# Cross-attention in a Perceiver layer: the value products of two groups done together in every second group

## What is computed

```python
x = x + _L0_xattn_ref(_layernorm(x), ctx_768, mask, Wq, Wk, Wv, Wo)   # x 32x64x512, ctx 32x512x384
    q = x @ Wq;  k = context @ Wk;  v = context @ Wv                  # 16 heads of 32
    attn = softmax(where(mask, q k^T * scale, -max))
    out = (attn @ v) @ Wo
x = x + _L0_attn_ref(_layernorm(x), ...)                              # causal self-attention with rope
x = x + _L0_ffn_ref(_layernorm(x), ...)                               # top half of the tokens, gelu, scatter
```

## Time and profile before

| | us |
|---|---|
| median of 3 runs | 1207.1 |
| the execution that was profiled | 1205.95 |
| its span, first to last instruction | 1204.2 |
| PE busy | 1184.5 (98%) |
| DVE busy | 752.1 (62%) |
| ACT busy | 623.7 (52%) |
| POOL busy | 600.5 (50%) |

### The profile page before, as it was taken

The page is one execution under the profiler, slowest core; times in us unless marked ns, Lnnn a source line. Parts: engine busy times, 40 slices in busy tenths (PEclk is TensorE's granted clock), DMA queues, the critical chain, the costliest instruction groups (busy, mean ns, idle before and its releaser), DMA issues.

```text
span 1204.2 us, 32635 instructions
## 1 busy us (share of the span) xinstructions
PE 1184.5 (98%) x12300; PEld 942.9 (78%) x12300; DVE 752.1 (62%) x1833; ACT 623.7 (52%) x1232; POOL 600.5 (50%) x331
## 2 busy tenths in 40 slices
PE   7999999999999999999999999999999998999997
PEld 6877777777777777777777777898888887888886
DVE  4256656756756666666666665458877899527323
ACT  6456556656656666566566557642232346433431
POOL 6922342532532523424424329467766663665763
PEclk9999999999999999999999999999999999999999
DMA  8145555555555555455455454201000113343431
GB/s 290 30 137 138 151 140 142 137 139 150 125 139 151 129 134 155 126 139 150 129 146 139 129 144 112 75 6 26 22 20 20 24 33 106 123 151 111 158 120 54
DMA packets 89314, 137.01 MB, mean 114 GB/s; under 512 B 20768, under 2 KB 25120, under 8 KB 89248
## 3 DMA queue, kind: packets, MB, share of 16 engines
q1 hardware_dynamic: 82208, 124.01, 36.7%
q10 hardware_dynamic: 5760, 7.87, 2.8%
q0 software_dynamic: 1280, 4.20, 1.0%
HBM read 63.39 MB, written 6.29 MB: 58 GB/s over the span
## 4 chain that ended last, share of the span: by engine, by line
PE 93%; DVE 3%; issue 1%; POOL 1%; DMA 1%; ACT 0%; SPq 0%; POOLq 0%; DVEq 0%
PE psum L220 44%; PE psum L1856 7%; PE psum L2174 7%; PE psum L1137 7%; PE psum L238 6%; PE psum L249 5%; PE psum L294 4%; PE psum L1165 3%; PE psum L1126 3%; PE psum L875 3%; PE psum L1178 1%; PE psum L1221 1%; DMA tok<-in_x 1%; PE psum L280 1%; PE psum L1158 1%
## 5 line engine op out<-in xcount | busy, mean ns | idle before, releaser
L418 DVE CUSTOM_DVE_ANT_0 prob<-psum,mbias 128x512 f32<-128x512 f32 x256 | 165.4, 684 | 202.6 <-PE psum L238 202.6
L336 ACT ACTIVATE prob<-prob,nmx 128x512 f32<-128x512 f32 x256 | 182.7, 715 | 102.1 <-DVE nmx L418 77.4
L342 ACT ACTIVATE prob<-prob,rinv 128x512 f32<-128x512 f32 x256 | 176.3, 712 | 0.0
L596 POOL TENSOR_SCALAR ctx_a<-ctx_r 128x1536 fp32r<-128x1536 f32 x16 | 65.5, 4095 | 216.5 <-DMA ctx_r<-in_ctx 196.4
L441 DVE STREAM_TRANSPOSE blocks<-prob 128x512 f32<-128x512 f32 x240 | 163.1, 699 | 12.6 <-ACT prob L342 12.6
L596 POOL TENSOR_SCALAR ctx_b<-ctx_r 128x1536 fp32r<-128x1536 f32 x16 | 65.5, 4092 | 186.5 <-PE psum L220 159.1
L367 ACT ACTIVATE V<-psum 128x512 f32<-128x512 f32 x120 | 71.7, 598 | 166.1 <-PE psum L220 166.1
L220 PE MATMUL psum<-ctx_b,wk_h 128*128 128x512 f32 x384 | 127.2, 398 | 0.0
L220 PE MATMUL psum<-ctx_a,wk_h 128*128 128x512 f32 x384 | 126.7, 398 | 0.0
L220 PE MATMUL psum<-wv_h,ctx_b 128*128 128x512 f32 x384 | 124.8, 391 | 0.2 <-DVE K L433 0.2
L220 PE MATMUL psum<-wv_h,ctx_a 128*128 128x512 f32 x384 | 124.2, 390 | 0.3 <-DVE K L433 0.3
(11 more groups left out here) (242 smaller groups left out, 2838.4 us busy)
## 6 DMA issues: line engine op xcount, KB each, us to landing
turned<-blocks SPq DMA_DIRECT2D x840, 64.0 KB
ctx_r<-in_ctx SPq DMA_DIRECT2D x32, 768.0 KB
w_r<-in_L_ffn_W SPq DMA_DIRECT2D x64, 256.0 KB, 2.8
turned<-blocks ACTq DMA_DIRECT2D x120, 64.0 KB
xres<-in_x SPq DMA_DIRECT2D x16, 256.0 KB
out<-tok SPq DMA_DIRECT2D x16, 256.0 KB, 2.0
pX<-squares SPq DMA_DIRECT2D x52, 64.0 KB, 2.0
tok<-in_x SPq DMA_DIRECT2D x3, 1024.0 KB, 12.0
```

Source lines behind the costliest of these rows:

```text
L336: act.activation(prob[:, r, :], prob[:, r, :], ACT.Exp, bias=nmx[:, r:r + 1], scale=-1.0, accum_out=rsum[:, r:r + 1]).then_inc(s_ex, 1)
L342: act.activation(prob[:, r, :], prob[:, r, :], ACT.Copy, scale=rinv[:, r:r + 1]).then_inc(s_pn, 1)
L418: dve.tensor_tensor_reduce(prob[:, r, :], S_bank[r], mbias[:, b, :], 1.0, 3.0e38, ALU.add, ALU.min, nmx[:, r:r + 1]).then_inc(s_mx, 1)
L596: pool.tensor_scalar(y[:, 0], ctx_r[:], 1.0, None, ALU.mult).then_inc(s_cx, 1)
```

## The change

In an odd group (q = 1 or 3) PE now does the value products of groups i - 3 and i - 2 one right behind the other (`values_of_two`), into the two halves of PV_bank; in an even group it does none, and goes from the scores to item 0. ScalarE and VectorE copy both results with one instruction each of 128x256 elements in the odd group, and none in the even one. ScalarE's two transfers for the even group are issued in the odd group after it, behind that copy and ahead of norm 0. SP's program is not edited; its wait for the value products of group i - 2 is one that, for an even i, is now met within group i + 1. `dve_blocks` waits for the landing of the exchange of two groups before (`s_ex4`) where it waited for the value products. The output projection and tile 15 are as they were.

```diff
+        def values_of_two(pe, g, q, first=False):
+            i, z = GPT * g + q, (q - 3) % GPT
+            for e in range(2):
+                pe.wait_ge(s_ex4[z + e], 256 * (g + 1 if q >= 2 else g))
+            if not (first and q == 3):
+                pe.wait_ge(s_Ol, i - 3)
+            for e in range(2):
+                value_products(pe, z + e, lambda c, kt, r: turned[e][:, 2 * c:2 * c + 2, r, kt, :],
+                               PV_bank[:, e * 2 * SQ:(e + 1) * 2 * SQ])
...
         def pe_group(pe, g, q, first=False):
             pe_scores(pe, g, q, first)
-            if not (first and q < 2):
-                pe_exchanged_values(pe, g, q, first)
+            if q % 2 and not (first and q == 1):
+                values_of_two(pe, g, q, first)
             pe_item(pe, g, q, 0)
...
+        def act_outputs_of_two(act, g, q, first):
+            act.wait_ge(s_PV, GPT * g + q - 1)
+            if q == 3 and not first:
+                act.wait_ge(s_Wo, g)
+            act.activation(outputs_of_two(OT_h, q), two_in_bank(), ACT.Copy).then_inc(s_Oh, 2)
+
+        def dve_outputs_of_two(dve, g, q):
+            dve.wait_ge(s_Oh, GPT * g + q - 1)
+            dve.tensor_tensor(outputs_of_two(OT_l, q), two_in_bank(), outputs_of_two(OT_h, q).bitcast(F32),
+                              ALU.subtract).then_inc(s_Ol, 2)
...
         def act_group(act, g, q, first=False):
             act_exp(act, g, q, 0)
             act_exp(act, g, q, 1)
-            if not (first and q < 2):
-                act_outputs(act, g, q, 2, first)
+            if q % 2 and not (first and q == 1):
+                act_outputs_of_two(act, g, q, first)
+                act_exchange(act, g, q - 1, first)
             act_norm(act, g, q, 0)
...
             act_item(act, g, q, 3)
-            act_exchange(act, g, q, first)
+            if q % 2 or (first and q == 0):
+                act_exchange(act, g, q, first)
...
             dve.wait_ge(s_pn, 4 * i + r + 1)
             if r == 0 and not (first and q < 2):
-                dve.wait_ge(s_PV, i - 1)
+                dve.wait_ge(s_ex4[(q - 2) % GPT], 256 * (g + 1 if q >= 2 else g))
...
             dve_inverse(dve, g, q, 1)
-            if not (first and q < 2):
-                dve_outputs(dve, g, q, 2)
+            if q % 2 and not (first and q == 1):
+                dve_outputs_of_two(dve, g, q)
             dve_blocks(dve, g, q, 0, first)
             dve_item(dve, g, q, 0)
```

More of the change, by code:

```diff
@@ L262, in pe_values, with pe_exchanged_values @@
             value_products(pe, z, lambda c, kt, r: PT[:, r, kt, c * SQ:(c + 1) * SQ], place)
-        def pe_exchanged_values(pe, g, q, first=False):
+        def pe_exchanged_values(pe, g, q):
             i, z = GPT * g + q, (q - 2) % GPT
             pe.wait_ge(s_ex4[z], 256 * (g + 1 if q >= 2 else g))
-            if not (first and q == 2):
-                pe.wait_ge(s_Ol, i - 2)
+            pe.wait_ge(s_Ol, i - 2)
             value_products(pe, z, lambda c, kt, r: turned[z % 2][:, 2 * c:2 * c + 2, r, kt, :], PV_bank)
@@ L354, in outputs_part, with outputs_of_two, two_in_bank, act_outputs @@
             return x[:, 2 * a:2 * a + 2, b, :]
-        def act_outputs(act, g, q, lag, first=False, place=PV_bank):
+        def outputs_of_two(x, q):
+            return x[:, :, (q - 3) % GPT // HALVES, :]
+        def two_in_bank():
+            return PV_bank[:, 0:4 * SQ].rearrange("p (c n) -> p c n", c=4)
+        def act_outputs_of_two(act, g, q, first):
[7 more added lines that the diff above has]
+                              ALU.subtract).then_inc(s_Ol, 2)
+        def act_outputs(act, g, q, lag, place=PV_bank):
             z = (q - lag) % GPT
             act.wait_ge(s_PV, GPT * g + q - lag + 1)
-            if z == 0 and not first:
+            if z == 0:
                 act.wait_ge(s_Wo, g)
```

## The result

The changed kernel takes 1228.53 us, the median of four runs (1228.36 to 1230.22), against 1207.08 for the kernel before on the same occasions: a ratio of 1.0183, with a 95% interval of 1.017 to 1.0196, +21.45 us. The forecast was 1226.5, slower.

A forecast was written before the change was run, and what follows sets the result against it. The prediction took PE to bound the kernel, with VectorE's copy of item 0 only 0.13 us ahead of it. Its terms, -9.0 + 11.8 + 15.6 + 2.0 = +20.4 us on 1205.95, gave 1226.5, range 1215 to 1243.

The forecast's parts named there:

- The prediction's first step: Item 2 on PE needs VectorE's copy of item 0, which ends 0.13 us before PE's load; starting sooner runs into it.
- Even groups: 29 groups losing value products: PE waits for the K copy, so each saves 0.31 us and not 1.03, -9.0 us.
- favourable bound of 9.96: Length in us of tile 0's group without value products, taken as an even group's best case, a saving of 0.47.
- Odd groups, q = 1: 14 groups gaining a second product, any late K copy covered by the output projection: +0.84 us each, +11.8 us.
- q = 3: 15 groups with a second product and norm 0 delayed by ScalarE's copy and issues: +1.04 us each, +15.6 us.
- my low end: For q = 3 groups: the delay stays hidden and only the second product's +0.84 us is paid.
- if the issues run beside the copy, norm 0 is 1.16 late: In q = 3, ScalarE's two DMA issues ahead of norm 0 delay it 1.16 us; behind the copy, 1.40.
- Exchanges: Exchange 3 lands just in time in middle tiles; 1.6 us late in tile 1, part of that in tile 2: +2.0 us.
- The wait of 0.1 in each of 14 tiles: Estimate with 2.0 us fixed cost per transfer: last landing at T3 + 22.7, 0.1 us late per tile, 1 us in all.
- Rival 1, the gain: The K copy doesn't bind in even groups; each pair saves 0.19 us, 5.4 us in all, to 1200.5; chance 0.05.
- rate of tile 0: SP's slower exchange issues, 0.73 us each; in all tiles they would cost 22 us, 1246, SP the bound; chance 0.11.

The follow-up runs named there:

- k_first_even: The changed kernel, but in even groups VectorE copies item 0 ahead of slot 0's transposition: 1219.39 us, ratio 1.0111.
- the two kernels with fewer products: The kernel before with a quarter of the value products in even groups: 1201.47 us; the same with item 0's copy ahead of slot 0's transposition there: 1186.46 us.
- scalar_issues_at_end: The changed kernel, but ScalarE issues its two transfers of the even exchange at the odd group's end, which also delayed exp 0 of even groups: 1254.02 us, ratio 1.0403.
- the run with three transfers on ScalarE: k_first_even_xres_early with item 0's copy before slot 3's maximum in even groups and ScalarE issuing three transfers of odd exchanges, not two: 1216.17 us, ratio 1.0076.
- k_first_even_xres_early: k_first_even, with SP loading the residual rows ahead of exchange 2 and not between exchanges 2 and 3: 1213.07 us, ratio 1.0055.
- both_k_first: k_first_even_xres_early, with item 1's copy too ahead of a transposition, slot 1's, in even groups: 1208.77 us, ratio 1.0019.

## Why the prediction was right, and where its terms were off

**The bound and the mechanism.** The prediction's first step, that VectorE's copy of item 0 has 0.13 us of cover and anything that starts item 2 sooner runs into it, was seen in the chain of after and shown by three changes: k_first_even, the two kernels with fewer products, and the delayed exp 0.

**Even groups: forecast -9.0, measured -5.9.** The K copy ended at T + 5.86 (464.95 + 0.65 - 459.74) and not at T + 5.75. Norm 0 did start 0.16 sooner (463.47, T + 3.73); the transposition followed at 464.32, T + 4.58, 0.11 later than the earlier trace rows gives. The favourable bound of 9.96, taken from tile 0, holds for tile 0 alone: its q = 2 took 9.95.

**Odd groups, q = 1: forecast +11.8, measured +12.5 without tile 2's wait.** The second product costs 0.89, not 0.84: the pair 1.92, one group 1.03. I had taken the step between loads from a duration of 0.94; in the pair it is (1.83 - 0.11) / 127 = 0.0135 us, 0.87 for 64, and the rest is in the rounding and the change to the items.

**q = 3: forecast +15.6, measured +13.4 without tile 0's stall.** The case of my low end was the right one: the second product's 0.89 each and no wait for the copy. The step that failed is "if the issues run beside the copy, norm 0 is 1.16 late": the sequencer ran ahead by more, and began the first issue beside exp 1. The run scalar_issues_at_end shows that with the issues gone from there (norm 0 at T + 3.9) the group is no shorter.

**Exchanges: forecast +2.0, measured 1.5, and with 1.0 from another cause.** The timetable was near: SP at T3 + 2.3 where I had 2.4, the last issue at T3 + 20.3 where I had 20.7, its landing 2.0 later where I had 1.8. In k_first_even, whose SP works to the same times, exchange 3 landed at 486.04, T3 + 22.3, and PE went on at T3 + 22.5, where I had it hidden by 0.1; with the even group 0.6 shorter PE waited 0.5. But the wait of the first tiles came in tile 2's q = 1 and not in tile 1's: the slow row of issues was tile 1's exchange 2, 10.44 us, while in tile 0 PE's own stall put its request off by 1.0. The 1.0 is the stall in tile 0, which no step of mine had. The landing itself, which no row of before gave, is on record in the trace of after (DMA from issue to landing, 488 issues of SP and 68 of ScalarE):

```profile
DMA to landing us min/median/max: 1.9/2.0/3.2
```

The Trainium skill's 2.0 us of fixed cost ("DMA: Bandwidth & Descriptors", anatomy of one DMA) agrees with that median, though the page fitted it for the software path. My 1.8 was read from the DMA engines' share, which doesn't show when a landing is told. The wait of 0.1 in each of 14 tiles that this figure gave in the prediction didn't come, since SP's row was 0.4 quicker than I had reckoned: the one wait for a transfer is tile 2's.

**Rival 1, the gain.** It is real and half as large. With both copies first a tile without waits takes 44.23 us in place of 44.45, so a pair of groups costs 0.11 us less than before, not 0.19. By the Trainium skill ("TensorEngine Tiling (Array Packing)", Key Properties) a change of tiling mode drains TensorE; the runs agree in sign, with 0.1 us for what a pair saves, but none of them shows a drain apart from the rest.

**How near, and how much of it by luck.** The errors of the terms are +3.1, +0.7, -2.2 and, with the last tile's 0.3, +0.8. +20.4 was forecast, +22.65 is what the profiled executions show in these groups and +21.45 what the medians show. That the sum lies so near is in part luck: the error of the even groups and that of q = 3 cancel, and a stall that no step had stands in for part of the forecast waits. And 1226.5 is the sum on top of the profiled execution; on top of the median of 1207.1 it would have been 1227.5.

## What to carry to other kernels

Before you take work away from the engine that bounds a kernel, look up the next instruction of that engine that waits for another one, and by how much it was in time. Here 0.13 us of cover stood against 1.03 us of work removed, and the other engine's order, slot 0's transposition ahead of a copy that could run 1 us sooner, decided the result. Where a change gathers waits into every second round, reorder the helpers first, and give the queue that now starts late (SP's row of issues at 0.64 us each) nothing to carry that can go sooner.

## What the runs showed of the hardware that I had not expected

**A stall of PE behind the first pair.** In tile 0's q = 3, which is straight code and has the first pair of 128 records in 1.9 us, PE stood still after the first matmul of item 0, waiting for nothing that the profile shows: 0.69 us in after, 1.3 in k_first_even, 1.9 in the run with three transfers on ScalarE, 2.2 in k_first_even_xres_early, 2.4 in both_k_first, none where tile 0 did its products singly. The chain of both_k_first there:

```profile
99.72 1.93 PE psum L260 x128
101.65 0.42 PE psum L220
102.07 2.39 issue
104.47 9.83 PE psum L220 x35
```

The 35 matmuls behind it take 9.83 us where they take 8.23 in after. The windows of the same kernel (busy time by engine, then PEclk, DMA share, GB/s) say why:

```profile
102.00:104.00 2.00, 0.07 (x1) 0.00 (x0) 1.07 (x5) 1.05 (x4) 2.00 (x1) 1.00 0.44 108
104.00:106.00 2.00, 1.53 (x4) 1.25 (x5) 0.71 (x1) 2.00 (x5) 1.88 (x1) 0.64 0.55 137
106.00:108.00 2.00, 2.00 (x7) 1.52 (x6) 0.00 (x0) 0.23 (x2) 1.93 (x1) 0.50 0.17 40
108.00:110.00 2.00, 2.00 (x10) 1.66 (x9) 1.41 (x4) 1.02 (x2) 1.92 (x2) 1.00 0.41 101
```

PE was idle for nearly all of 102 to 104; then the granted clock fell to 0.50, the lower of its two levels (1.2 GHz), until 108, and came back while PE worked. It fell behind the stalls of 1.9, 2.2 and 2.4 us and stayed at 1.00 behind those of 0.69 and 1.3. So a stall of 2.4 us cost 4 us. In after, a packet of the instruction queue (packets, MB, share) is moved between 102.5 and 103.5, just ahead of the stall at 104.14:

```profile
q8 instruction: 1, 0.02, 6.0%
```

In all seven kernels with a pair in tile 0 such a packet starts 2.3 to 2.4 us before PE goes on (102.52 and 104.83 in after, 102.09 and 104.47 in both_k_first), whether PE has stood 0.7 us by then or 2.4. That PE waited for its instructions is likely by this, and not shown: nothing was tried on it alone.

**SP's slow issues come with the same packets.** Nearly all of SP's exchange issues take about 0.59 us. Five of the 840 in after take 0.97 to 1.89, all in tiles 0 and 1, and each overlaps a packet of the instruction queue; the two in tile 1's exchange 2 make its row of 10.44. The six slowest of before (1.30 to 1.63) overlap one as well, and between 155 and 745 us there is neither. So the "rate of tile 0" of the prediction is a few single long issues. That the packet is the cause is not shown.

**ScalarE's DMA issues overlap its own work.** The two issues of 0.53 and 0.62 us in the middle of the softmax put norm 0 at T + 4.57 where it is at 3.90 without them, 0.67 for 1.15 us of issues, since the first began while exp 1 ran; the wider copy alone makes up the other 0.11. Four issues at the start of a softmax, which ended at T + 2.8, put exp 0 at T + 3.2 where it was at 2.3.
